# Running sums over edges in a graph network: one VectorE instruction per edge column, or a scan over 12 columns (6 where rows are wide)

## The reference

```python
def _segment_sum(src, seg, n):
    return jax.ops.segment_sum(src, seg, n)
# attention, layer L2
e = jax.nn.leaky_relu(a_s[src] + a_d[dst], NEG_SLOPE)
m = jax.ops.segment_max(e, dst, num_segments=n)
p = jnp.exp(e - m[dst])
z = jax.ops.segment_sum(p, dst, num_segments=n)
alpha = p / (z[dst] + EPS_SOFTMAX)
msg = h[src] * alpha[:, :, None]
out = jax.ops.segment_sum(msg, dst, num_segments=n)
```

## The kernel before

| pass | kind | floats per row | gathers, us from the start |
|---|---|---|---|
| 0 | attention, 8 heads | 152 | 188.9 to 1333.3 |
| 1 | plain, with the degree | 129 | 1538.2 to 2621.0 |
| 2 | plain, wide | 256 | 2787.3 to 3871.0 |
| 3 | plain | 128 | 4090.3 to 5172.4 |
| 4 | attention, 4 heads | 140 | 5401.8 to 6529.6 |
| 5, 6, 7 | weighted | 128 | from 6801.1, 8002.1, 9204.4 |

## Time and profile before

### The profile page before, as it was taken

One profiled execution on the slowest core, in us unless ns is written; L12 is line 12 of the kernel. 1 busy time (PEld: TensorE's weight loads), 2 busy tenths in 40 slices (PEclk: granted clock), 3 DMA queues, 4 the chain that ended last, 5 costly groups with the idle time before them and its releaser, 6 DMA issues. The chain is left out here.

```text
span 10433.9 us, 25725 instructions
## 1 busy us (share of the span) xinstructions
PE 421.8 (4%) x2048; PEld 303.3 (3%) x2048; DVE 3439.7 (33%) x8044; ACT 1484.0 (14%) x3624; POOL 6862.1 (66%) x6765
## 2 busy tenths in 40 slices
PE   2000000000300004000010000000001000000000
PEld 1000000000200002000010000000000000000000
DVE  4444452222233331222234444622222222222223
ACT  1000001001121111100000000022221222212221
POOL 4666637777477763777656666177775777667774
...
GB/s 97 106 104 108 101 58 98 94 94 92 106 194 188 187 171 57 96 93 93 87 51 100 95 99 102 26 96 98 94 93 79 96 93 93 88 86 94 93 93 72
DMA packets 359329, 1035.33 MB, mean 99 GB/s; under 512 B 118369, under 2 KB 200010, under 8 KB 323178
## 3 DMA queue, kind: packets, MB, share of 16 engines
q0 software_dynamic: 242832, 506.98, 18.4%
...
## 5 line engine op out<-in xcount | busy, mean ns | idle before, releaser
L262 POOL DMA_INDIRECT gb<-rows,src x6256 | 6375.9, 1019 | 3005.6 <-issue 1968.1
L355 DVE SCALAR_TENSOR_TENSOR gb<-gb,mask,psum 128x128 f32<-128x128 f32 (+1 forms) x4686 | 1733.1, 370 | 4668.5 <-remote 1903.8
L337 ACT ACTIVATE psum<-gb,weight 128x128 f32<-128x128 f32 x2346 | 837.1, 368 | 2463.7 <-issue 1724.3
L1079 DVE SCALAR_TENSOR_TENSOR gb<-gb,mask,psum 128x136 f32<-128x136 f32 (+1 forms) x1492 | 527.6, 354 | 621.0 <-DVE gb L1079 339.5
L339 ACT COPY psum<-gb 128x512 f32<-128x512 f32 (+2 forms) x823 | 423.0, 561 | 1858.0 <-DMA gb<-rows,src 1554.2
L279 POOL DMA_INDIRECT gb<-runs,end_row x392 | 375.6, 958 | 154.0 <-issue 117.1
L1074 DVE TENSOR_TENSOR psum<-gb,psum 128x408 f32<-128x408 f32 (+4 forms) x546 | 306.8, 562 | 242.3 <-DVE gb L1079 149.8
L1008 ACT ACTIVATE psum<-running 128x192 f32<-128x192 f32 (+3 forms) x72 | 20.7, 288 | 2346.0 <-DVE running L1064 2173.8
L364 PE MATMUL psum<-gb,carry_from 128*128 128x128 f32 (+2 forms) x12 | 5.2, 534 | 6795.1 <-DVE gb L355 6795.1
L646 POOL DMA_INDIRECT spread<-acc,spread_row x98 | 94.4, 963 | 228.7 <-DVE spread_row L917 118.1
L364 PEld LDWEIGHTS psum<-gb,carry_from 128*128 128x128 f32 x12 | 3.0, 310 | 6796.6 <-DVE gb L355 5509.9
...
...
## 6 DMA issues: line engine op xcount, KB each, us to landing
...
gb<-rows,src POOLq DMA_INDIRECT x6256
...
```

What stands on the lines that cost most here:

```text
L262: m.s_rows[b % BUFS].up(nc.gpsimd.indirect_dma_start(m.batch(b, columns, row)[:, j, 0:width], None, table, bass.IndirectOffsetOnAxis(ap=m. ...
L337: last = nc.scalar.activation(out[:, j - j0, :], rows[:, j, 0:width], ACT.Copy, scale=m.weight[:, r:r + 1])
L355: m.s_column.up(nc.vector.scalar_tensor_tensor(rows[:, j, 0:width], before, m.mask[:, r:r + 1], fed[:, j - j0, :], ALU.mult, ALU.add))
L1079: m.s_column.up(nc.vector.scalar_tensor_tensor(rows[:, j, 0:S], before, m.mask[:, r + j:r + j + 1], fed[:, j - j0, :], ALU.mult, ALU.add))
```

## The change

The columns of a batch are cut into parts of SCAN columns: 12 and 11 in a narrow batch, 6, 6 and 5 in a wide one. For each part

- ScalarE copies the rows from `gb` into half of PSUM (four banks) with the feature outside and the column inside ("by feature"), so that the columns of one feature are neighbours (L399; one ACTIVATE per column, L397, in weighted passes). It reads with the row's stride, 512 B, 516 B or 1024 B, and writes contiguously; L397 reads contiguously and writes at a stride of 48 or 44 B.
- ScalarE spreads the mask of the part's columns over all features, beside the sums, in `tmp` (L401); `begun` is the mask with 0 at each part's first column.
- VectorE adds the carry from the part before into column 0 of each feature (L418) and runs one scan over the whole part (L423): mask from SBUF, sums from PSUM, result into SBUF.
- ScalarE lays the result back by column over the gathered rows (L377), contiguous read and a row's stride in writing. This stands in its program behind the feed and the mask of the next part.

A store waits for the lay-back (`s_laid`) instead of `s_column`, and POOL no longer waits for a column. An attention pass does the same with one PSUM area, one area for the sums (`turn`) and one for the mask: the products are made by feature (L1183), then carry (L1187) and scan (L1194), and ScalarE lays back and spreads the next mask. `begun` is made anew before each pass. The number of VectorE instructions falls from 23 to 4 for a narrow plain or weighted batch, from 17 to 6 for a wide one.

```diff
--- before.py
+++ after.py
...
 NARROW, WIDE = 23, 17
 assert COLS % NARROW == 0 and COLS % WIDE == 0
+SCAN = {NARROW: 12, WIDE: 6}
 ENDING = {NARROW: (12, 7, 4), WIDE: (9, 5, 3)}
 
 
...
@@ -256,7 +262,6 @@
         if b >= BUFS:
             stored = m.s_run_stored[b % BUFS]
             pool.wait_ge(stored.sem, stored.at(16 * (b // BUFS)))
-            pool.wait_ge(m.s_column.sem, m.s_column.at(batches[b - BUFS + 1][0] + 1))
         for j in range(size):
             r = first + j
             m.s_rows[b % BUFS].up(nc.gpsimd.indirect_dma_start(
@@ -284,7 +289,7 @@
 
     edges = by_edge(runs)
     for b, (first, size) in enumerate(plan(columns)):
-        sp.wait_ge(m.s_column.sem, m.s_column.at(first + size))
+        sp.wait_ge(m.s_laid.sem, m.s_laid.at(scans_by(columns, b)))
         if put:
             sp.wait_ge(m.s_put.sem, m.s_put.at(b + 1))
         m.s_run_stored[b % BUFS].up(sp.dma_start(edges[:, first:first + size, :], m.batch(b, columns, width)[:, 0:size, :]), 16)
@@ -298,68 +303,129 @@
     engine.wait_ge(rows.sem, rows.at(16 * landed_by(columns, b)))
 
 
+def portions(columns):
+
     found = []
     for b, (first, size) in enumerate(plan(columns)):
+        for j in range(0, size, SCAN[columns]):
+            found.append((b, first, j, min(j + SCAN[columns], size)))
     return found
 
 
+def scans_by(columns, b):
+
+    return sum(1 for n, *_ in portions(columns) if n <= b)
+
+
+def begin_scans(m, c, columns):
+
+    c.link(m.nc.vector.tensor_copy(m.begun[:, :], m.mask[:, 0:COLS]))
+    whole = (COLS // columns - 1) * columns
+    starts = [m.begun[:, 0:whole].rearrange("p (b j) -> p b j", j=columns)[:, :, 0:columns:SCAN[columns]]]
+    starts += [m.begun[:, first + j:first + j + 1] for _, first, j, _ in portions(columns) if first >= whole]
+    for at in starts:
+        m.s_scan_mask.up(m.nc.vector.memset(at, 0.0))
+
+
...
+def by_feature(flat, count, width):
+
+    return flat[:, 0:count * width].rearrange("p (w j) -> p w j", j=count)
+
+
...
+HALF = 4
...
+class Scans:
+    def __init__(self, m, columns, width, row):
+        self.m, self.columns, self.width, self.row = m, columns, width, row
+        self.parts = portions(columns)
+        self.flat = m.tmp[:, :, :].rearrange("p t d -> p (t d)")
+
+    def fed(self, n):
+        _, _, j0, j1 = self.parts[n]
+        return self.m.psum[:, n % 2 * HALF:n % 2 * HALF + HALF, :].rearrange("p b c -> p (b c)")[:, 0:(j1 - j0) * self.width]
+
+    def area(self, k, n):
+        _, _, j0, j1 = self.parts[n]
+        at = (2 * k + n % 2) * SCAN[self.columns] * self.width
+        return self.flat[:, at:at + (j1 - j0) * self.width]
+
...
+    def last(self, n):
+        _, _, j0, j1 = self.parts[n]
+        return self.by_feature(self.area(1, n), n)[:, :, j1 - j0 - 1]
+
+    def lay(self, act, n):
+        m = self.m
+        b, _, j0, j1 = self.parts[n]
+        act.wait_ge(m.s_summed.sem, m.s_summed.at(n + 1))
+        m.s_laid.up(m.nc.scalar.copy(m.batch(b, self.columns, self.row)[:, j0:j1, 0:self.width].rearrange("p j w -> p w j"),
+                                     self.by_feature(self.area(1, n), n)))
+
+    def act(self, act, weighted, marks, last_column=None):
+        m, nc = self.m, self.m.nc
+        act.wait_ge(m.s_scan_mask.sem, m.s_scan_mask.at(marks))
+        for n, (b, first, j0, j1) in enumerate(self.parts):
+            rows = m.batch(b, self.columns, self.row)
+            if j0 == 0:
+                wait_batch(m, act, b, self.columns)
+                if last_column is not None:
+                    size = plan(self.columns)[b][1]
+                    m.s_put.up(nc.scalar.copy(rows[:, 0:size, self.width], last_column[:, first:first + size]))
+            if n >= 2:
+                act.wait_ge(m.s_summed.sem, m.s_summed.at(n - 1))
+            out = self.by_feature(self.fed(n), n)
+            if weighted:
+                for j in range(j0, j1):
+                    r = first + j
+                    m.s_fed.up(nc.scalar.activation(out[:, :, j - j0], rows[:, j, 0:self.width], ACT.Copy, scale=m.weight[:, r:r + 1]))
+            else:
+                m.s_fed.up(nc.scalar.copy(out, rows[:, j0:j1, 0:self.width].rearrange("p j w -> p w j")), 1)
+            r = first + j0
+            m.s_masked.up(nc.scalar.copy(self.by_feature(self.area(0, n), n),
+                                         m.begun[:, r:r + j1 - j0].unsqueeze(1).broadcast_to([P, self.width, j1 - j0])))
+            if n:
+                self.lay(act, n - 1)
+        self.lay(act, len(self.parts) - 1)
+
+    def dve(self, dve, weighted):
+        m, nc = self.m, self.m.nc
+        fed = 0
+        for n, (b, first, j0, j1) in enumerate(self.parts):
+            fed += j1 - j0 if weighted else 1
+            dve.wait_ge(m.s_fed.sem, m.s_fed.at(fed))
+            if n:
+                dve.wait_ge(m.s_summed.sem, m.s_summed.at(n))
+                before = self.last(n - 1)
+                one = self.by_feature(self.fed(n), n)[:, :, 0]
+                r = first + j0
+                m.s_begun.up(nc.vector.scalar_tensor_tensor(one, before, m.mask[:, r:r + 1], one, ALU.mult, ALU.add))
+                dve.wait_ge(m.s_begun.sem, m.s_begun.at(n))
+            dve.wait_ge(m.s_masked.sem, m.s_masked.at(n + 1))
+            if n >= 2:
+                dve.wait_ge(m.s_laid.sem, m.s_laid.at(n - 1))
+            m.s_summed.up(nc.vector.tensor_tensor_scan(self.area(1, n), self.area(0, n), self.fed(n), 0.0, ALU.mult, ALU.add))
 
 
 def carry_sums(m, pe, columns, width, row):
 
-    pe.wait_ge(m.s_column.sem, m.s_column.at(COLS))
+    pe.wait_ge(m.s_laid.sem, m.s_laid.at(len(portions(columns))))
     end = row_before(m, len(plan(columns)), columns, row)[:, 0:width]
     m.s_carry.up(m.nc.tensor.matmul(m.psum[:, 2, 0:width], m.carry_from[:, :], end, start=True, stop=True))
 
...
@@ -964,10 +1038,24 @@
         return factor.unsqueeze(2).broadcast_to([P, H, C + 1])
 
     prob_flat, reset_flat = m.psum[:, 7, 0:H * (B + 1)], m.psum[:, 7, H * (B + 1):2 * H * (B + 1) + 1]
-    most = 512 // S
+    parts = portions(B)
+    fed_flat = m.psum[:, 0:HALF, :].rearrange("p b c -> p (b c)")
+    m_turn = m.turn[:, :, :, :].rearrange("p a b c -> p (a b c)")
+    scan_mask = m.gb[:, BUFS * WIDE * HID - SCAN[B] * S:BUFS * WIDE * HID]
+
+    def fed(n):
+        return by_feature(fed_flat, parts[n][3] - parts[n][2], S)
+
+    def summed(n):
+        return by_feature(m_turn, parts[n][3] - parts[n][2], S)
+
...
+    def last_summed(n):
+        return summed(n)[:, :, parts[n][3] - parts[n][2] - 1]
+
+    last_row = last_summed(len(parts) - 1)
...
@@ -1002,11 +1090,27 @@
         @block.scalar
         def _(act):
             head.act(act)
+            def expand(n):
+                _, first, j0, j1 = parts[n]
+                m.s_masked.up(nc.scalar.copy(by_feature(scan_mask, j1 - j0, S),
+                                             m.begun[:, first + j0:first + j1].unsqueeze(1).broadcast_to([P, S, j1 - j0])))
+
+            if head.first:
+                act.wait_ge(m.s_prepared.sem, m.s_prepared.at(1))
+            else:
+                act.wait_ge(m.s_scan_mask.sem, m.s_scan_mask.at(MARKS[B]))
+            expand(0)
             for b, (first, size) in enumerate(plan(B)):
                 K = size + 1
                 act.wait_ge(m.s_logits.sem, m.s_logits.at(b + 1))
                 m.s_probs.up(nc.scalar.activation(prob_flat[:, 0:H * K], m.running[:, 0:H * K], ACT.Exp))
                 m.s_put.up(nc.scalar.copy(m.batch(b, B, W)[:, 0:size, S:S + H].rearrange("p j h -> p h j"), heads_of(m.top, K)[:, :, 1:K]))
+                for n, (at, _, j0, j1) in enumerate(parts):
+                    if at == b:
+                        act.wait_ge(m.s_summed.sem, m.s_summed.at(n + 1))
+                        m.s_laid.up(nc.scalar.copy(m.batch(b, B, W)[:, j0:j1, 0:S].rearrange("p j w -> p w j"), summed(n)))
+                        if n + 1 < len(parts):
+                            expand(n + 1)
             act.wait_ge(m.s_logits.sem, m.s_logits.at(batches + 1))
             m.s_probs.up(nc.scalar.activation(end_factor, end_factor, ACT.Exp))
             act.wait_ge(m.s_logits.sem, m.s_logits.at(batches + 2))
...
@@ -1063,22 +1169,31 @@
                                                     -BIG, ALU.add, ALU.max))
                 m.s_logits.up(nc.vector.tensor_tensor(m.running[:, 0:L], m.logit[:, 0:L], m.top[:, 0:L], ALU.subtract))
                 dve.wait_ge(m.s_probs.sem, m.s_probs.at(b + 1))
...
+                if b == 0:
                     c.link(nc.vector.memset(m.carried[:, 0:S], 0.0))
...
+                for n, (at, _, j0, j1) in enumerate(parts):
+                    if at != b:
+                        continue
+                    begin = fed(n)[:, :, 0]
+                    if n:
+                        before = last_summed(n - 1)
+                        dve.wait_ge(m.s_summed.sem, m.s_summed.at(n))
+                        if j0 == 0:
```

(14 more changed lines are left out.)

87 lines of the change are left out of this document (26 added, 61 removed).

## The result

On the chip of the first measurement the changed kernel took 10367.71 us (10365.60 to 10368.28, 5 runs) against 10415.89 us: ratio 0.9953, 95% interval [0.9938, 0.9967], faster by 48 us where I had forecast 116. The profiled execution has a span of 10,365.9 us, 68 less than before; of the sum of 115, which is counted in span too, that is 59%. (The profiled execution before lay 20 us above its median; 68 less 20 is the 48.)

What follows compares the result with a forecast made beforehand. POOL's gathers were taken as the bound, 1.40 us each after some 180. Terms of -130 attention, -46 plain, +121 wide and -60 weighted gave -115; 10,436 - 115 - 20 = 10,301, said as 10,300; range 9,940 to 11,000.

Steps and rivals of the forecast that it cites:

- the sum of 115: All passes: -130 attention, -46 plain, +121 wide, -60 weighted, set against the profiled execution of 10,436 us.
- Reading P: POOL: each engine has its own instruction supply, one per 1.40 us during gathers, after a stock for some 180; 60%.
- -70 and -60 foretold: Attention passes 0 and 4: stops go, POOL falls to 1.40 us per gather; 70 and 60 us less.
- Rival 3 (S): POOL slows only because another engine issues constantly; passes 0, 1, 3, 4 keep 1.25 us per gather; 9,940 us, 20%.
- the step that took 2.4 ns per element for a stride of 1024 B: Wide pass: feed and lay-back at this price make ScalarE set the pace, 26.3 us a batch, +121 us.
- rival 2: Wide pass: 1024 B stride costs 2.1 ns or less, -23 instead of +121 us; 10,157 us in all, 20%.
- The -23 that rival 2 adds for the pass end: Wide pass: the stop ahead of the last gathers and most of the sums behind them go, -23 us.
- a stop gives POOL its 1.25 pace back, so I take the present 32.2 us a batch: Weighted passes: 27 ScalarE instructions a batch need few stops, between 28.8 and 33.6 us; no change from the present.
- its -20 for the pass end: Weighted passes 5, 6, 7: the stop and most sums at the pass end go, -20 us each, -60 together.
- -46 foretold: Plain passes 1 and 3: the stop ahead of the last gathers and most sums behind go, about -23 us each.
- Rivals 4 and 5: Wide pass: 1024 B dearer, 10,780 or 11,260 us, 22%; scans slow gathers, 10,760, 4%; weighted batches 37.8 us, 10,870, 4%.

Runs made afterwards that it cites:

- no_sums_d: The changed kernel with feed, mask, scan and lay-back left out of passes 1 and 3: 10,349.96 us where the kernel before takes 10,416.
- lay_first_d: The changed kernel with the lay-back of a batch's last part ahead of the wait for the next batch: 10,356.0 us beside 10,416.9 before.

## Why the prediction was wrong

The time, 10,368, lies in the range; the forecast of 116 us faster was more than twice the measured 48, from terms that missed by up to 121 us in both directions.

- **What bounds the kernel.** Reading P was right on chip A: 1.40 us per gather comes without any work on VectorE and almost none on ScalarE (no_sums_d). What I took for "a supply of instructions" is a description, not a cause: what sets 1.40 us, and why only on some chips, stays open. I could not know from one chip's trace that the spacing was the chip's and not the kernel's.
- **Attention passes.** -70 and -60 foretold, -69.6 and -56.0 measured; the mechanism (stops go, POOL falls to 1.40) shows in the windows. What I had not costed is the end of the pass: without stops POOL ends a long unbroken run of gathers, and the instructions behind it are spaced as during it. The first gather behind pass 4 (L279) starts 24.2 us after the last instead of 13.9. +7.0 and +12.6 us behind passes 0 and 4; on a chip B it is +4.3 and +2.3, so about 3 and 10 us of them are the spacing and the rest the new work. Rival 3 (S) is out.
- **Wide pass: the step that took 2.4 ns per element for a stride of 1024 B failed.** It is 1.7 for the feed and 1.8 for the lay-back, as at 512 B, and ScalarE has idle time; rival 2 had that part right, -0.4 instead of +121. The row at 608 B was no accident (L1111 has 2.3 to 2.5 at 608 B and 1.7 at 560); what failed is to carry it on to 1024 B by distance. The Trainium skill, "Advanced Engine Details and Errata", Memory Cachelines, has a penalty where each access goes to a different line. The equal prices at 512 and 1024 B agree with it; the higher one at 608 B it does not explain, and its cause is open. The -23 that rival 2 adds for the pass end did not come either: 16.4 us of stops remain. One of 4.3 goes with the lay-backs first, the other of 12.1 does not (12.0 in lay_first_d; 16.4 before), so the order is not its cause.
- **Weighted passes: the step "a stop gives POOL its 1.25 pace back, so I take the present 32.2 us a batch", and its -20 for the pass end, failed.** The pace does come back (all gathers 0.95 us), but 15 stops of 9 us cost more than it gives. ScalarE takes the 37.8 us a batch that I had worked out and set aside wherever it is behind, and so POOL's batches come as four of 28.8 us and three of 35 to 38. That is 32.6 on average over a pass of 1107.9 us, where the kernel before had 32.0, because its first seven batches ran at 28.8 (1087.8 us with its stop of 20.8 at the end). The stop that I took off at the end is still there, 16.8 + 5.4 us in pass 5. So each pass is 17 to 19 us longer ahead of its end, 1 to 4 us at its end, and 5 to 8 us shorter behind it: +45 in place of -60. That the lay-back's order causes it, which I held possible afterwards, is refuted (lay_first_d); the count of ScalarE's instructions fits to 0.1 us in the trace, but a run with fewer of them on chip A is missing.
- **Plain passes.** -46 foretold; the gathers gave -20, 5 us short at each end because of the late lay-back. Behind pass 1 the first gather (L279) comes 8 us sooner, as in my sum, but 15 us are lost again in the dense part, where VectorE's waits for the products add up to 115.4 us (L548, the longest 44.5) instead of 100.3 (L482). On a chip B the two kernels need 115 and 116 us behind pass 1, here 166 and 173. Why the waits grew is open.
- **Rivals 4 and 5.** The stride of 1024 B was no dearer, the scans leave the gathers alone: 737.82 us busy in the weighted pass on a chip B (737.79 before). A weighted batch of 37.8 us did come, in two or three batches of seven; what ScalarE gains in the stops keeps it from coming in all.

The two large misses, 121 us too much for the wide pass and 105 too little for the weighted ones, cancelled but for 16 us, and that was luck. The attention and the plain passes gained 24 and 39 us less than foretold; 24 + 39 - 16 are the 47 us between -115 and -68. That the time lies in the range says little for the sum.
